# A twelve-layer decoder kernel: when a stage's weights are fetched, and where a stage's last statistics and output stand in the next stage

## The reference

```python
x = _layernorm(x + _L0_ffn_ref(...))     # stage 2: routed slots with a GRU
x = _layernorm(x + _L1_attn_ref(...))    # stage 3: linear attention over the sequences
...
x = _layernorm(x + _L2_attn_ref(...))    # stage 6: relu attention without softmax
x = _layernorm(x + _L2_xattn_ref(...))   # stage 7: softmax attention to a context, 16 heads of 8, then an MLP
x = _layernorm(x + _L2_ffn_ref(...))     # stage 8: eight linear experts, the best two of them
x = _layernorm(x + _L3_attn_ref(...))    # stage 9: rotary, causal softmax attention, 16 heads of 64
x = _layernorm(x + _L3_xattn_ref(...))   # stage 10: softmax attention to a context, 16 heads of 8
```

## Time and profile before

| | |
|---|---|
| median of 3 timed runs | 3165.18 us (3158.66 to 3166.9) |
| the profiled execution | 3162.29 us, of it the span of the trace 3160.5 us |
| TensorE (PE) busy | 2699.9 us, 85% |
| VectorE (DVE) busy | 1929.2 us, 61% |
| ScalarE (ACT) busy | 1378.0 us, 44% |
| GpSimd (POOL) busy | 1365.7 us, 43% |
| mean granted TensorE clock | 0.908 of full speed |
| stage 2 to 3, 6 to 7, 8 to 9, 9 to 10 (first work of the next stage) | about 840, 1942, 2285 and 2831 us |

### The profile page before, as it was taken

How to read it: one execution, slowest core, us unless ns; L and a number is a source line. 1 busy time by engine, 2 the same in 40 slices (tenths; PEclk the granted TensorE clock), 3 DMA queues, 4 the chain that set the end, 5 groups by cost and what they waited for, 6 DMA issues and landing times. The chain is left out here.

```text
span 3160.5 us, 78251 instructions
## 1 busy us (share of the span) xinstructions
PE 2699.9 (85%) x31745; PEld 1918.1 (61%) x31745; DVE 1929.2 (61%) x5041; ACT 1378.0 (44%) x3100; POOL 1365.7 (43%) x1474
## 2 busy tenths in 40 slices
PE   7894665576779997999999987998889999988986
PEld 4552343354446775565999975666357777765665
DVE  7888999255664443666544444664856665645665
ACT  4553555263445653444322223552134444435554
POOL 4773666173311213444233343553833333424656
PEclk9997767787779998999899997997989999999998
DMA  3000000400000001000000000001000000000000
GB/s 107 2 2 1 1 1 1 119 1 1 7 19 17 2 2 42 3 3 4 7 1 1 1 1 17 2 2 45 1 6 2 2 2 2 2 9 2 2 4 25
DMA packets 25795, 37.15 MB, mean 12 GB/s; under 512 B 760, under 2 KB 22656, under 8 KB 24576
## 3 DMA queue, kind: packets, MB, share of 16 engines
q1 hardware_dynamic: 25440, 32.16, 3.4%
HBM read 29.93 MB, written 2.23 MB: 10 GB/s over the span
## 5 line engine op out<-in xcount | busy, mean ns | idle before, releaser
L1499 POOL TENSOR_TENSOR L_attn__qk<-L_attn__turned 128x512 f32<-128x512 f32 x128 | 161.5, 1272 | 308.9 <-DVE L_attn__turned L1619 308.9
L4660 PE MATMUL psum<-L_ffn__e_hT,weights 128*128 128x256 f32 x1024 | 244.5, 382 | 0.0
L1033 DVE TENSOR_REDUCE L_xattn__nm<-psum 128x8 bf16<-128x1024 f32 x128 | 156.4, 1224 | 141.7 <-PE psum L1249 135.3
L1619 DVE TENSOR_TENSOR L_attn__turned<-psum,weights 128x1024 f32<-128x1024 f32 x128 | 153.3, 1219 | 95.1 <-PE psum L1736 92.9
L4660 PEld LDWEIGHTS psum<-L_ffn__e_hT,weights 128*128 128x128 f32 x1024 | 186.6, 192 | 20.6
L4507 DVE TENSOR_TENSOR L_ffn__e_a<-L_ffn__e_sg,psum 128x512 f32<-128x512 f32 x128 | 88.1, 689 | 176.2 <-ACT L_ffn__e_sg L4499 176.1
L4499 ACT ACTIVATE L_ffn__e_sg<-psum 128x512 f32<-128x512 f32 x128 | 76.4, 597 | 258.7 <-PE psum L4660 258.7
L966 ACT ACTIVATE L_xattn__pT<-psum 128x1024 f32<-128x1024 f32 x128 | 124.1, 1021 | 58.7 <-PE psum L1277 58.7
L1736 PE MATMUL psum<-L_attn__xT,weights 128*128 128x256 f32 x512 | 138.1, 405 | 10.0 <-DVE L_attn__turned L1619 9.5
L4673 PEld LDWEIGHTS psum<-weights,L_ffn__e_a 128*128 128x128 f32 x1024 | 134.4, 191 | 7.2 <-DVE L_ffn__e_a L4507 0.7
L4673 PE MATMUL psum<-weights,L_ffn__e_a 128*128 128x128 f32 x1024 | 135.0, 275 | 0.5 <-DVE L_ffn__e_a L4507 0.5
(11 more groups left out here) (682 smaller groups left out, 7547.5 us busy)
## 6 DMA issues: line engine op xcount, KB each, us to landing
L_xattn__conv_toeplitz<-s4d_kernel SPq DMA_DIRECT2D x5, 1024.0 KB, 12.0
weights<-pack SPq DMA_DIRECT2D x1, 3328.0 KB, 12.7
weights<-pack SPq DMA_DIRECT2D x1, 3140.0 KB, 10.1
weights<-s4d_kernel SPq DMA_DIRECT2D x3, 1024.0 KB, 9.1
L_attn__bias_tables<-pack SPq DMA_DIRECT2D x1, 2048.0 KB, 10.1
out_dram<-X SPq DMA_DIRECT2D x8, 256.0 KB, 2.3
weights<-pack SPq DMA_DIRECT2D x1, 1603.5 KB, 14.9
ctxT<-ctxT_in SPq DMA_DIRECT2D x1, 1536.0 KB, 10.6
```

Source lines behind the costliest of these rows:

```text
L1033: nc.vector.tensor_reduce(nm[:, n % 2, :].rearrange("p (g c) -> p g c", g=4)[:, 2 * u:2 * u + 2, 0:4], scores[u].rearrange("p g (i q) -> p ...
L1499: nc.gpsimd.tensor_tensor(qk[:, p % 2, u], turned[:, g % 2, :, 0:2 * P], turned[:, g % 2, :, 2 * P:4 * P], ALU.add).then_inc(qk_sb, 1)
L1619: nc.vector.tensor_tensor(turned[:, g % 2], proj[u % 2].unsqueeze(1).to_broadcast([P, 2, 4 * P]), k.w(name + "rope").rearrange("p (t q) -> ...
L4660: last = nc.tensor.matmul(bank[g % 2][:, 256 * c:256 * c + 256], k.w(name + w)[:, o:o + P], hT, start=True, stop=True)
```

## The change

Fetches: stage 2 no longer waits at all before it fetches stage 3's weights, and stage 6 waits for stage 5.5's `weights_read` in place of its own last projection.

`attention8` (stages 7 and 10): POOL's `late_pool` goes behind both masks of pair 0 and `with_bias(0)`; ACT's `late_act` behind `exponentials(0)`; on DVE `late_dve` is now the residual alone (for stage 6), the statistics are a new `middle_dve` behind `maxima(0)`, and `last_dve` (`shifted`) stands behind `maxima(1)`. Stage 9's ending has residual and statistics together in `late_dve` as before, and its `late_pool` is the whole of `normed(15)`.

`attention64_rope` (stage 9, behind stage 8): POOL's `late_pool` behind all eight additions; DVE's `late_dve` behind `maxima(0)` and `last_dve` behind the first product with the reciprocals (`weighted(0)`); ACT's `late_act` behind the evictions of n = 0. The copy of the masks goes from DVE to ACT, before the casts; DVE waits for POOL's `zeroed` only before `maxima(0)`. The evictions of V wait for stage 8's last sums on POOL (`sums_added`) in place of `x_out`; the first `weigh` waits for `sums_read`; and stage 8's buffers are laid out in another order, so that those still in use are not written over.

```diff
@@ attention8, POOL
-                if before:
-                    before.late_pool(pool)
                 pool.wait_ge(k.loaded[stage], 16)
...
                     mask_queries(0)
                     pool.wait_ge(bo_sb, 1)
                     with_bias(0)
+                    if before:
+                        before.late_pool(pool)
@@ attention8, ACT
                 evict_v(0)
-                if before:
-                    before.late_act(act)
                 evict_x(1)
...
                     exponentials(n)
+                    if before and n == 0:
+                        before.late_act(act)
@@ attention8, DVE
-                if before:
-                    before.last_dve(dve)
...
                 dve.wait_ge(zeroed, 1)
                 maxima(0)
+                if before:
+                    before.middle_dve(dve)
...
                         maxima(n + 1)
+                    if before and n == 0:
+                        before.last_dve(dve)
@@ attention64_rope, POOL
                 for u in range(UNITS):
-                    if u == 4:
-                        before.late_pool(pool)
                     add_turned(0, u)
+                before.late_pool(pool)
@@ attention64_rope, ACT
                 evict_x(0)
+                nc.scalar.activation(
+                    masks[:], k.w(name + "masks").rearrange("p (a g q) -> p a g q", a=2, g=4).unsqueeze(3)
+                    .to_broadcast([P, 2, 4, 4, P]), ACT.Copy).then_inc(masks_sb, 1)
                 for u in range(UNITS):
                     cast(0, u)
-                before.late_act(act)
-                act.wait_ge(before.x_out, NB // 4)
+                act.wait_ge(*before.sums_added)
                 for i in range(4):
                     evict_v(0, i)
...
                     evict_over(n)
+                    if n == 0:
+                        before.late_act(act)
@@ attention64_rope, DVE
-                dve.wait_ge(zeroed, 1)
-                nc.vector.tensor_copy(
-                    masks[:], ...
                 for u in range(UNITS):
                     turn(0, u)
-                    if u == 3:
-                        before.late_dve(dve)
-                    if u == 6:
-                        before.last_dve(dve)
+                dve.wait_ge(zeroed, 1)
                 maxima(0)
+                before.late_dve(dve)
...
                         weighted(n)
+                        if n == 0:
+                            before.last_dve(dve)
@@ attention64_rope, PE, weigh(n)
+                    if n == 0:
+                        pe.wait_ge(*before.sums_read)
@@ attention_relu, SP
-                sp.wait_ge(y_ps, UNITS)
+                sp.wait_ge(*before.weights_read)
                 k.load_weights(sp, k.next_stage(stage))
@@ attention_relu, ending
                 def late_dve(dve):
                     residual(UNITS - 1)
+
+                def middle_dve(dve):
                     statistics(UNITS - 1)
@@ experts_linear
-        ending = Ending(x_out, 2, (res_sb, UNITS), (part_sb, UNITS))
+        ending = Ending(x_out, 2, (b_ps, UNITS), (prod_sb, 2 * NB))
+        ending.sums_added, ending.sums_read = (quarter_sb, NB), (part_sb, UNITS)
```

More of the change, by code:

```diff
@@ L1662, in _ @@
                 dve.wait_ge(k.loaded[stage], 16)
-                dve.wait_ge(zeroed, 1)
-                nc.vector.tensor_copy(
-                    masks[:], k.w(name + "masks").rearrange("p (a g q) -> p a g q", a=2, g=4).unsqueeze(3)
-                    .to_broadcast([P, 2, 4, 4, P])).then_inc(masks_sb, 1)
                 for u in range(UNITS):
                     turn(0, u)
-                    if u == 3:
-                        before.late_dve(dve)
-                    if u == 6:
-                        before.last_dve(dve)
+                dve.wait_ge(zeroed, 1)
                 maxima(0)
+                before.late_dve(dve)
                 for n in range(NB):
@@ L1704, in late_dve @@
                     residual(NB - 1)
-                ending.late_dve, ending.last_dve = late_dve, lambda dve: None
+                ending.late_dve, ending.middle_dve, ending.last_dve = late_dve, lambda dve: None, lambda dve: None
             @block.tensor
@@ L2443, in last_dve @@
                     shifted(UNITS - 1)
-                ending.late_dve, ending.last_dve = late_dve, last_dve
+                ending.late_dve, ending.middle_dve, ending.last_dve = late_dve, middle_dve, last_dve
             @block.tensor
@@ L4707, in event @@
             return sig.one(what, 1, 1).sem
-        XT = sb("xT", [P, NB, P])
+        part, r = sb("part", [P, 4, DM]), sb("r", [P, 2, 4, DM])
+        st, mv = sb("st", [P, 4, 6]), sb("mv", [P, 2, 4, 2])
+        rstd, shift = sb("rstd", [P, 2, 2, 4]), sb("shift", [P, 2, 4])
+        quarter = sb("quarter", [P, 2, 2, 4, DM])
         L, W, second = sb("L", [P, NB, NE]), sb("W", [P, NB, NE]), sb("second", [P, HALF, NE])
@@ L4713, in experts_linear @@
         wT = sb("wT", [4 * NE, 2, P])
-        prod, half = sb("prod", [P, 3, NE, DM]), sb("half", [P, 2, 4, DM])
-        quarter = sb("quarter", [P, 2, 2, 4, DM])
-        part, r = sb("part", [P, 4, DM]), sb("r", [P, 2, 4, DM])
-        st, mv = sb("st", [P, 4, 6]), sb("mv", [P, 2, 4, 2])
-        rstd, shift = sb("rstd", [P, 2, 2, 4]), sb("shift", [P, 2, 4])
+        half, prod = sb("half", [P, 2, 4, DM]), sb("prod", [P, 3, NE, DM])
+        XT = sb("xT", [P, NB, P])
         XA, LG, B, WT = k.bank[0:2], [k.bank[3], k.bank[2]], k.bank[3], k.bank[1]
```

## The result

| | before | after |
|---|---|---|
| median of 6 timed runs of each, side by side | 3160.61 us (3152.73 to 3166.9) | 3134.1 us (3127.98 to 3139.18) |
| ratio, 95% interval | | 0.9917 [0.9903, 0.993] |
| the profiled execution, of it the span | 3162.29, 3160.5 us | 3129.11, 3127.3 us |

So the change takes 26.3 us (22 to 31) off. The forecast was 3144 and the range 3134 to 3153; 3134.1 lies 0.1 us inside its lower end.

A forecast was written before the change was run, and what follows sets the result against it. TensorE is busiest on average, but the fills at the joints, where it waits, were taken as what the change touches. Terms 1.9 + 2.2 + 12.5 + 4.8 = 21.4 us off 3165.2 gave 3144 us, range 3134 to 3153.

The forecast's parts named there:

- joint 2 to 3: Slots to linear attention: with the weights fetched early, the last block_out and all behind it come 1.9 us sooner.
- joint 6 to 7: Relu attention to cross attention: early weights and moved tail give 4.4 us, ACT's new wait takes half back: 2.2 us.
- joint 8 to 9: Linear experts to rotary attention: masks on ACT, VectorE's earlier turns and moved tails give 12.5 us, bounds 9.5 and 14.6.
- joint 9 to 10: Start of stage 10: both masks ahead of normed(15) bring the maxima 4.3 us sooner, fuller clock 0.5: 4.8 us.
- the one of full clock in the fills (3136): Rival: clock full from the middle of each fill and ACT's new wait covered, 29 us; chance of below 3139: 0.11.
- the loops between are not: Only the fills at the joints are touched, not the loops between, so each joint's gain reaches the end one for one.
- ACT begins at 841.6: Joint 2 to 3: with the weights there, ACT begins its two units at 841.6 in place of 843.88.
- 4.4 us at the first exponentials: Joint 6 to 7: stage 7's first exponentials come at about 1954.4 in place of 1958.79.
- TensorE has nearly unbroken work: Joint 8 to 9: TensorE's nearly unbroken work from 2294 on was the reason for taking 12.5 us from 9.7 to 13.
- the prediction's signs of being wrong: Wrong if a loop's period changes, stage 9's first additions wait for TensorE, or ACT's stage 7 wait exceeds 4 us.
- it may keep full clock, 0 to -3: Joint 9 to 10: TensorE's shorter wait before the first scores may keep full clock, 0 to 3 us, taken at 0.5.
- The slower rival: VectorE meets POOL on every turn of a loop; at 1.7 us a turn in stage 9, 3199 us; chance 0.03.

The follow-up runs named there:

- after_again: The changed kernel, unaltered, measured and profiled once more in a second set of 6 runs: 3131.29 us, 0.9904 of the kernel before.
- better: Changed kernel with stage 7's shifted(7) directly behind the statistics, and POOL's root of stage 8's unit 6 and nm behind the eight additions: 3129.74 us, ratio 0.9901.

## Why the prediction was right, and where it was not

| step | predicted | by the stretches |
|---|---|---|
| joint 2 to 3 | 1.9 | 1.4 to 1.6 (1.0 where the low clock fell on it) |
| joint 6 to 7 | 2.2 | 3.7 |
| joint 8 to 9 | 12.5 | 13.0 to 13.1 |
| joint 9 to 10 | 4.8 | 3.0 (moves alone) to 4.1 (whole change) |
| sum | 21.4 | 21 to 22.5 |

- The sum of the edits came out, in part by luck: joint 6 to 7 gave 1.5 us more than its term and joint 9 to 10 up to 1.8 less. The 10 us between 3144 and 3134.1 are not in it. 4.6 us are the base: the forecast counts from 3165.2, the median of three runs, and six gave 3160.6. The rest lies in stretches that nobody edited: 2.0 us in stage 8 and 1.0 us in the joint behind it, both by the low clock, and some 2 us that no single profile places (some 6 by the second set of runs). One place where they may lie, though no run shows it, is queries(0) to LP6: seven of the eight kernels with the early fetches took 1088.4 to 1088.7 us there and one 1084.3; of the six without, four took 1090.2 to 1090.5 and two 1087.0 and 1087.1. Of the rivals, the one of full clock in the fills (3136) comes nearest in time, yet not for its reason: ACT's wait wasn't covered, stage 7's start ran at 0.50, and stage 10 did in the kernel after from its first exponentials on.
- What the prediction had at nothing is that "the loops between are not" touched "so what a joint gives goes to the end one for one". The loops kept their periods, but stage 8, of which the change moves nothing ahead of T9, took 1.9 to 3.1 us less in eight of the nine kernels with stage 7's moves and in none of the five without. That it is the moves' doing through the clock is likely, not shown.
- Joint 2 to 3: the step "ACT begins at 841.6" failed. Behind the weights stood TensorE's transposes, which ran at the low level (28 of them in 5.82 us, before 4.29), so ACT began at 843.00, 3.2 us behind the last projection, where the prediction had 2.6.
- Joint 6 to 7: 4.4 us at the first exponentials was right (4.55: from LP6 to E7.0 18.74 us before, 14.19 after), the wait was there, and the term mis-sized is what it takes back: 2.2 us predicted at the second exponentials, 0.6 measured there (8.56 us behind the first, before 7.93) and 0.8 at the fourth. The second maxima began 2.19 us behind the exponentials, not 3.3, as the granted clock was 0.91 over the 4 us behind the first exponentials, where it had been 0.51 before. With fetches and moves taken apart, 3.4 belong to the load, and the moves add 0.1 alone and 0.3 in the whole.
- Joint 8 to 9: the chain was right link by link: turns from 2.2 us behind T9, eight additions as the bound, ended 17.0 us behind T9 (17.8 in `after_again`; predicted 17.4 to 18.6, ideal 16.2), ACT's 3.2 us away and free in their new place (first to second exponentials 15.78 us, before 15.79), the tails in idle time (VectorE's ended at 2299.6 and it idled 2.80 us after them), masks 3.61 us on ACT with no cast waiting. That "TensorE has nearly unbroken work" and so keeps its clock was half right: the low level came for 3.4 us among the additions (6.8 in `after_again`) and for 3.4 from behind the first maxima on, where it had come for 24 of the first 42 us before. Two additions waited 0.42 and 0.50 us for turns that had themselves waited for TensorE: of the prediction's signs of being wrong, a small piece of one.
- Joint 9 to 10: the move gives 4.54 us at the maxima (predicted 4.3). What failed is "it may keep full clock, 0 to -3": the fill did run at full clock, which gave 1.2 us up to the first exponentials in the kernel after (3.97 against 5.20), but the low level came later, for 13.6 us from the first exponentials on, and took 1.5 to 2.1 us back by the fourth. And the profiled execution before had 3.0 us of low clock ahead of R that eleven of the others have not.
- The slower rival (a loop in which VectorE meets POOL on every turn) didn't come: both loops kept their length to 0.2 us in all fourteen kernels, as the trace's silence on such meetings inside them let expect.

## What to carry to other kernels

Count a joint from mark to mark and ask which chain ends last; a step moved out of it is worth its duration only on that chain, and here that held within 1 us for 13. Where TensorE waited, its clock often went low a while later, over work: in the kernel after it idled 2.6 us among stage 9's turns and ran the next ones at 0.50, and in `better`, where it idled about 1 us there, the clock stayed at 1.00. So a gain at the start of a fill may come back as a slower stretch behind it, and taking a wait away can lengthen that stretch (1.2 us gained and 2.1 lost in stage 7 of `better`): judge a joint by the loop's steady state behind it. Compare stretches that repeat to 0.1 us in place of runs that differ by 10, and profile the kernel before twice before resting a step on a row.

## What the hardware showed beyond that

- VectorE's plain copy of 128x128 (`bvw`) took 2.56 us at 1935.26, where the same copy took 0.22 us at 2807.19; POOL's memset of 128x2560 (2.23 us) ran beside it from 1935.51 and ended at 1937.74, with it 1937.82. The Trainium skill (SBUF — State Buffer, Who interferes with whom) blocks VectorE's fast copy modes while GpSimd uses the port; these rows agree, and show it for an operation of GpSimd that only writes. All eight kernels with the early fetches have the 2.56 us there; in the six without, the copy came behind the memset and took 0.23. It cost nothing here: VectorE's next product came from TensorE at 1941.01.
- `score` (8 matrix products for n = 0) took 1.14 us at full clock and 2.09 us at 0.50 (2814.47 and 1945.53 in the kernel after).
- Stages 7 and 10 begin with stretches at 0.50 in every kernel, and they go on while TensorE is busy without a gap (4.00 of 4.00 us at 0.50 in `better`). A longer one is at the start of stage 8 in the kernel before: from 2181 to 2204 us TensorE was busy 23.00 of 23.00 us, at 0.50.
